# Products on constants in the waits of TensorE, wider landmark products and a later transposition, in a four-layer transformer kernel

## The chip, the cores and the metric

The kernel runs on one core of a Trainium2 chip. The metric is the device time of one execution in microseconds (us), lower is better. TensorE is called PE below, VectorE DVE, ScalarE ACT, GpSimd POOL and SyncE SP.

## What is computed

The input x has 4 sequences of 512 rows of 128 numbers, all in fp32. Six residual layers follow each other:

```python
x = x + 0.5 * L0_ffn(layernorm(x))    # 8 dense experts of 128 hidden units, weights from a sigmoid router
x = x + L0_attn(layernorm(x))         # 16 heads of 8, 64 landmarks, 6 Newton steps for an inverse
x = x + 0.5 * L0_ffn(layernorm(x))
x = x + 0.5 * L1_ffn(layernorm(x))    # 32 experts, top 4 of each row, and 4 shared experts
x = x + L1_attn(layernorm(x))         # windows of 128 keys, 7 windows a sequence
x = x + 0.5 * L1_ffn(layernorm(x))
```

The inverse of the landmark attention starts from V = K^T / denom, where denom is the largest column sum, and repeats V = 0.25 V (13 I - KV (15 I - KV (7 I - KV))). Its result is multiplied with the landmark rows of kernel3 @ v.

## The kernel before

The 2048 rows are held as 16 tiles of 128 rows, in four groups of 512 (one group is one sequence). Every engine has its instructions written out in a fixed order, and semaphores are waited for by hand; whatever stands behind a wait in an engine's order waits too. The program has these stages, with the times at which they lie in the profiled execution:

- **Dense feed-forward, first (0 to 102 us)**, function `ffn0`. 32 steps, eight experts for each of four groups. In step s, PE does `gate_up(s + 1)` (six products of 512 columns, L404 to L406), then what else is due in that step, and then `down(s)` (L1324), which waits for DVE's `hidden(s)` (L1237). ACT applies silu and scales the result (L1196), POOL adds it to x (L1122). Routing and normalising (L215) of later groups are pieces in DVE's order, put between two `hidden`. `FOLLOWING` says at which step of the next group the norm of the next stage is done for a finished group.
- **Landmark attention (102 to 307 us)**, `attn0`. After the scores of the landmarks come six Newton iterations for all heads (`times`, L1939, products of 72 columns: 64 of the matrix A and, behind them, 8 of the landmark rows), then `landmark_values` (L1979), products of the 8 last columns alone. With them go `scores1` (L1956), whose row maxima DVE takes (L1770), `turn_maxima` (L1991), and the scores and values of all rows (L2002, L2015, L2018).
- **Dense feed-forward, second, with the routing of the sparse layer (307 to 473 us)**, `ffn0` with `srt`. For each finished group the norm, the router and the ranks of its rows are worked out in steps of the next group (`SOON`, `SPREAD`), and POOL then sends the rows to `sorted_rows` in DRAM by 16 indirect transfers a group (`pool_dispatch`, L455). Their list also has the `power` (L208) on which the norm of the next group waits. Steps 32 to 47 are the shared experts.
- **Tiles of the sparse layer (473 to 607 us)**, `Sorted.tiles`: 20 quads of four tiles. SP and ACT load them, PE transposes (L894), multiplies (L916), transposes (L923), multiplies (L930), DVE weights the rows (L854) and POOL sends them back with four indirect transfers a quad (L731).
- **Window attention with the routing of the last layer (607 to 731 us)**, `attn1`, and **tiles again (731 to 860 us)**, then the last sums and the store.

Two helpers fill waits of PE with products whose result nobody reads:

```python
def keep_busy(n, b):
    for _ in range(n):
        PE.matmul(b[:, 0:3 * D], ident[:, :], wqkv[:, :], start=True, stop=True)
def keep_warm(n, b):
    for _ in range(n):
        PE.matmul(b[:, 0:P], ident[:, :], ident[:, :], start=True, stop=True)
```

They are the lines L176 and L180 of the profile. One product of fp32 is two instructions there, so `keep_busy(1)` is "x2" of L176 and `keep_warm(1)` is "x2" of L180. Both stand in PE's order ahead of a wait.

## Time and profile before

| | us |
|---|---|
| time, median of 3 runs | 877.46 |
| the three runs | 875.30, 877.46, 881.89 |
| the profiled execution | 880.06 |
| its span in the trace | 878.6 |
| mean granted clock of PE | 0.931 |

The span is from the first to the last instruction of the program; 1.5 us of the execution's time lie around it. "PEclk" or "granted clock" is the share of 2.4 GHz that PE's array was allowed to run at. It takes two values in this trace, 1.00 (2.4 GHz) and 0.50 (1.2 GHz); a value between the two is a mean over a stretch that has both. "Idle before" with an arrow names what ended the wait of an engine.

### The profile page before, as it was taken

The page shows a single profiled execution, that of the slowest core. Times are in us where ns is not written, and L with a number is a line of the kernel's source. Part 1 is how long each engine was busy: PE and PEld are TensorE (multiplying, and loading weights), DVE is VectorE, ACT ScalarE, POOL GpSimd, SP SyncE. Part 2 cuts the span into 40 slices and gives each one's busy share as a digit, 9 for nine tenths or more (in the row PEclk, how much of TensorE's full clock was granted, in tenths as well). Part 3 has the DMA queues.
Part 4 walks back from the last instruction along what each step waited for, and adds up shares of the span by engine and source line. Part 5 has one row for each costly group of instructions (what it writes and reads, how often), then busy time and mean ns, then how long its engine had stood idle before and what let it go on. Part 6 is the DMA issues. An engine that isn't in the chain of part 4 may idle for free.

```text
span 878.6 us, 19350 instructions
## 1 busy us (share of the span) xinstructions
PE 724.0 (82%) x6670; PEld 556.0 (63%) x6670; DVE 530.4 (60%) x1596; ACT 401.5 (46%) x971; POOL 446.0 (51%) x489
## 2 busy tenths in 40 slices
PE   7889998889999898888998677875888987788830
PEld 6778856569977567777776455553666774555520
DVE  6975596558856287867782354443876662354524
ACT  3657654556425455455413355640554323455520
POOL 4755530435500046375673367775357771477770
PEclk9999998999978998899999999997998998899985
DMA  9999999480045091011111444425001112344417
GB/s 229 214 216 217 217 214 219 97 160 4 5 101 111 1 324 37 1 46 37 44 56 52 107 105 109 107 79 209 1 31 54 56 57 50 86 109 111 111 52 245
DMA packets 121024, 93.98 MB, mean 107 GB/s; under 512 B 14176, under 2 KB 111840, under 8 KB 120544
## 3 DMA queue, kind: packets, MB, share of 16 engines
q1 hardware_dynamic: 104256, 70.00, 36.1%
q0 software_dynamic: 9216, 19.68, 6.5%
q10 hardware_dynamic: 7456, 3.07, 1.7%
q8 instruction: 54, 0.88, 0.4%
q14 instruction: 42, 0.34, 0.1%
HBM read 31.76 MB, written 57.41 MB: 101 GB/s over the span
## 4 chain that ended last, share of the span: by engine, by line
PE 39%; POOL 16%; DVE 15%; issue 12%; SPq 9%; ACT 5%; DMA 4%; ACTq 1%; DVEq 0%; POOLq 0%
POOL sorted_rows L455 8%; SPq L713 7%; POOL expert_rows L731 7%; PE banks L1939 5%; PE banks L1324 4%; PE banks L404 2%; PE banks L405 2%; PE banks L406 2%; PE banks L916 2%; DVE hT L1237 2%; PE banks L642 1%; PE banks L176 1%; PE banks L1956 1%; PE banks L1900 1%; DVE rows_x L215 1%
## 5 line engine op out<-in xcount | busy, mean ns | idle before, releaser
L731 POOL DMA_INDIRECT expert_rows<-y,goal x160 | 153.2, 957 | 103.9 <-DVE y L854 55.7
L455 POOL DMA_INDIRECT sorted_rows<-rows_x,row_of x128 | 126.4, 987 | 67.2 <-issue 37.2
L1196 ACT ACTIVATE ys<-banks,wtab 128x128 f32<-128x128 f32 x256 | 73.1, 370 | 65.2 <-PE banks L1324 53.5
L916 PE MATMUL banks<-routed_w,t 128*64 x320 | 83.0, 403 | 11.0 <-issue 5.5
L404 PE MATMUL banks<-x_high,w_high 128*128 128x512 f32 x192 | 86.1, 449 | 0.4 <-POOL w_low L1075 0.4
L1324 PE MATMUL banks<-w,hT 128*128 128x128 f32 x512 | 75.2, 293 | 11.1 <-DVE hT L1237 10.9
L916 PE MATMUL banks<-routed_scratch,t 128*64 128x256 f32 x320 | 83.1, 403 | 0.0
L1122 POOL TENSOR_TENSOR x<-ys,x 128x512 f32<-128x512 f32 x43 | 55.5, 1290 | 54.3 <-ACT ys L1196 54.0
L1324 PEld LDWEIGHTS banks<-w,hT 128*128 128x128 f32 x512 | 69.0, 203 | 20.2 <-DVE hT L1237 17.7
L406 PE MATMUL banks<-x_high,w_low 128*128 128x512 f32 x192 | 77.6, 404 | 0.0
L405 PE MATMUL banks<-x_low,w_high 128*128 128x512 f32 x192 | 77.1, 402 | 0.0
L763 ACT COPY routed_scratch<-routed_w 128x384 f32 x160 | 69.8, 509 | 11.2 <-issue 9.0
L208 POOL TENSOR_TENSOR rstd<-rstd,mhalf 128x4 f32<-128x4 f32 x24 | 25.6, 1065 | 96.3 <-DVE rstd L202 96.1
L916 PEld LDWEIGHTS banks<-routed_w,t 128*64 128x64 f32 x320 | 42.5, 143 | 37.2 <-issue 22.3
L1237 DVE TENSOR_TENSOR hT<-sg,banks 128x512 f32<-128x512 f32 x64 | 43.8, 684 | 30.0 <-ACT sg L1204 27.7
L823 DVE COPY t<-banks 128x512 f32<-128x512 f32 x38 | 26.2, 689 | 58.2 <-PE banks L894 54.4
L776 ACT COPY hT<-banks 128x512 f32<-128x512 f32 x38 | 22.2, 585 | 76.4 <-PE banks L923 59.6
L842 DVE TENSOR_TENSOR h<-sg,banks 128x512 f32<-128x512 f32 (+1 forms) x42 | 27.7, 659 | 36.9 <-ACT sg L770 22.1
L1939 PE MATMUL banks<-routed_w 64*64 64x72 f32 x1536 | 48.9, 223 | 0.6 <-DVE routed_w L1755 0.6
L1939 PEld LDWEIGHTS banks<-routed_w 64*64 64x64 f32 x1536 | 48.3, 133 | 1.2 <-DVE routed_w L1755 1.0
L176 PE MATMUL banks<-wqkv,ident 128*128 128x384 f32 x96 | 37.8, 542 | 11.9 <-DMA xnT<-expert_rows 8.9
L930 PE MATMUL banks<-routed_w,hT 128*64 x320 | 44.7, 283 | 1.8 <-ACT hT L776 1.8
(342 smaller groups left out, 1720.4 us busy)
## 6 DMA issues: line engine op xcount, KB each, us to landing
sorted_rows<-zeros SPq DMA_DIRECT2D x32, 1120.0 KB, 17.3
tile<-sorted_rows SPq DMA_DIRECT2D x252, 35.0 KB, 2.0
routed_w<-in_ffn_w SPq DMA_DIRECT2D x8, 768.0 KB, 11.4
w<-in_ffn_w SPq DMA_DIRECT2D x20, 192.0 KB, 5.6
expert_rows<-y,goal POOLq DMA_INDIRECT x160
tile<-sorted_rows ACTq DMA_DIRECT2D x68, 35.0 KB
qS<-x_high SPq DMA_DIRECT2D x8, 256.0 KB, 6.5
sorted_rows<-rows_x,row_of POOLq DMA_INDIRECT x128
```

The source lines that it names most:

```text
L404: PE.matmul(ps, expert.high[:, n, :], x_high[:, cols], start=True, stop=False)
L405: PE.matmul(ps, expert.high[:, n, :], x_low[:, cols], start=False, stop=False)
L406: return PE.matmul(ps, expert.low[:, n, :], x_high[:, cols], start=False, stop=True)
L455: POOL.indirect_dma_start(sorted_rows, bass.IndirectOffsetOnAxis(self.row_of[:, g, i:i + 1], 0), rows_x[:, 4 * g + i // TOPK, :], None).th ...
L713: SP.dma_start(tile[q % 3][ROWS * h:ROWS * h + ROWS, i, :], sorted_rows[bass.ds(row, ROWS), :]).then_inc(*(head_loaded if q == 0 and i > 1 ...
L731: POOL.indirect_dma_start(expert_rows, bass.IndirectOffsetOnAxis(goal[:, 4 * q + i:4 * q + i + 1], 0), y[q % 6][:, i * P:(i + 1) * P], Non ...
L763: last = SCL.copy(odd[q % 3][:, i, :], routed.w[:, bass.ds(expert[4 * q + i], 1), :].rearrange("p o c -> p (o c)"))
L916: last = PE.matmul(pairs(q)[ROWS * h:ROWS * h + ROWS, i, :], t[q % 2][:, rows], weights(q, i, h, slice(0, 2 * P)), start=True, stop=True)
L1196: last = SCL.mul(ys[s % 2][:, j * P:(j + 1) * P], bank[4 + s % 2][:, j * P:(j + 1) * P], wtab[:, t, e:e + 1])
L1237: DVE.tensor_tensor(hT[s % 2][:, :], sg[s % 2][:, :], bank[2 + s % 2][:, :], ALU.mult).then_inc(*hidden_done.inc)
L1324: last = PE.matmul(bank[4 + s % 2][:, j * P:(j + 1) * P], hT[s % 2][:, j * P:(j + 1) * P], experts[s % rows].w[:, 2, :], start=True, stop= ...
L1939: last = PE.matmul(bank[2 * b + k // 4][r, c + cols.start:c + cols.stop], X[r, k, 0:M], X[r, k, cols], start=True, stop=True)
```

## The change

- `Norm.transposes` gets a number of `keep_busy` products, which come after the wait for the free bank and ahead of the wait for the normalised rows. Two are given for group 3 in the second `ffn0`, and 0, 2, 1, 1 for the four groups of the sorted norm there. Elsewhere it is 0 and only the order of its two waits changes.
- `down` of `ffn0` waits for `scaled_done` first, then does 12 `keep_warm` products at step 6 of the first `ffn0` or 18 at step 9 of the second, and then waits for `hidden_done`.
- `FOLLOWING` for group 0: normalised at step 6 in place of 4 of the next group, transposed at 8 in place of 5, copied at 9 in place of 6.
- `landmark_values` multiplies with all 72 columns. The sequences and heads are laid out in reverse order, so that the 64 columns too many of each product fall on places that hold nothing yet or are written again by a later product. `rden`, `evict_w` and the reader of `WV` follow the new layout.
- `keep_busy` is put into `attn0` (1 and 2 products around the second `turn_maxima`, 1 ahead of the last `spread1`, 1 ahead of the last `output`), into both executions of `tiles` (5 in place of 2 ahead of the first tiles, 2 ahead of the second half of quad 0, 3 ahead of quad 2, 2 ahead of quad 3) and into `attn1` (22 in place of 10 at its start, 3 ahead of the last `srt.norm.transposes`).

```diff
@@ -215,10 +215,11 @@
 
-def transposes(self, g):
-    PE.wait_ge(*xn_ready(self.first + g + 1))
+def transposes(self, g, meanwhile=0):
     if self.turn[g]:
         PE.wait_ge(*xT_ready(self.turn[g]))
+    keep_busy(meanwhile, bank[6])
+    PE.wait_ge(*xn_ready(self.first + g + 1))
     for t in range(4):
@@ -934,9 +935,10 @@
         PE.wait_ge(*dispatched(4 * TOPK * NG))
-        keep_busy(2, bank[0])
+        keep_busy(5, bank[0])
         PE.wait_ge(*loaded(0))
         transposes(0, range(2))
+        keep_busy(2, bank[2])
         PE.wait_ge(*head_loaded(4))
@@ -957,6 +959,7 @@
         gate_up_rows(1, range(2, 4))
+        keep_busy(3, bank[1])
         PE.wait_ge(*loaded(2))
@@ -981,6 +984,8 @@
                 gate_up_rows(n, range(2, 4))
+            if n == 2:
+                keep_busy(2, bank[1])
             if n + 1 < QUADS:
@@ -1108,10 +1113,10 @@
 
-FOLLOWING = dict(statistics=1, normalised=4, transposes=5, copy=6)
+FOLLOWING = [dict(statistics=1, normalised=6, transposes=8, copy=9)] + [dict(statistics=1, normalised=4, transposes=5, copy=6)] * 2
 
 def following_at(s, piece):
-    return [g for g in range(NG - 1) if following and s == rows * (g + 1) + FOLLOWING[piece]]
+    return [g for g in range(NG - 1) if following and s == rows * (g + 1) + FOLLOWING[g][piece]]
 
@@ -1317,9 +1322,10 @@
             return srt.tensor_down(s, experts[8:12])
-        PE.wait_ge(*hidden_done(s + 1))
         if s > 1:
             PE.wait_ge(*scaled_done(s - 1))
+        keep_warm({9: 18}.get(s, 0) if srt else {6: 12}.get(s, 0), bank[4 + s % 2])
+        PE.wait_ge(*hidden_done(s + 1))
         for j in range(4):
@@ -1342,13 +1348,13 @@
         if s in transposes_at:
-            norm.transposes(transposes_at[s])
+            norm.transposes(transposes_at[s], 2 if srt and transposes_at[s] == 3 else 0)
         if s in logits_at:
...
         for g in groups_at(s, "transposes"):
-            srt.norm.transposes(g)
+            srt.norm.transposes(g, (0, 2, 1, 1)[g])
         for g in groups_at(s, "logits"):
@@ -1703,7 +1709,7 @@
             DVE.wait_ge(*rden_ready(b))
-            DVE.tensor_tensor(A[b - 1][:, :, 0:M], pv(bank[6]), m8(rden[:, b - 1, :]), ALU.mult).then_inc(*A_ready.inc)
+            DVE.tensor_tensor(A[b - 1][:, :, 0:M], pv(bank[6]), m8(rden[:, B - b, :]), ALU.mult).then_inc(*A_ready.inc)
         if b == B:
@@ -1718,8 +1724,8 @@
             DVE.wait_ge(*ksum_mm(b + 1))
-            DV(DVE.tensor_reduce(out=rden[:, b, :], in_=pv(bank2), axis=AX, op=ALU.max))
-            DVE.reciprocal(rden[:, b, :], rden[:, b, :]).then_inc(*rden_ready.inc)
+            DV(DVE.tensor_reduce(out=rden[:, B - 1 - b, :], in_=pv(bank2), axis=AX, op=ALU.max))
+            DVE.reciprocal(rden[:, B - 1 - b, :], rden[:, B - 1 - b, :]).then_inc(*rden_ready.inc)
 
@@ -1792,7 +1798,7 @@
         DVE.wait_ge(*W_mm(1))
-        w = bank[5][:, 0:B * NK * HD].rearrange("p (b k d) -> p b k d", b=B, d=HD)
+        w = bank[5][:, M:M + B * NK * HD].rearrange("p (b k d) -> p b k d", b=B, d=HD)
         for h, r in enumerate(HALF):
@@ -1973,10 +1979,10 @@
         PE.wait_ge(*turn(next_ready, 6, max(b, 2)))
-        for k in range(NK):
+        for k in reversed(range(NK)):
             for r in HALF:
-                c = b * GH * 2 + k * HD
-                last = PE.matmul(bank[5][r, c:c + HD], K[b][r, k, :], A[b][r, k, M:TC], start=True, stop=True)
+                c = ((B - 1 - b) * NK + k) * HD
+                last = PE.matmul(bank[5][r, c:c + TC], K[b][r, k, :], A[b][r, k, :], start=True, stop=True)
         if b == B - 1:
@@ -2012,7 +2018,7 @@
         for j in range(4):
-            PE.matmul(bank[5][GH * j:GH * j + GH, :], WV[:, b, 2 * j + c, :], e1[2 * j + c], start=c == 0, stop=c == 1)
+            PE.matmul(bank[5][GH * j:GH * j + GH, :], WV[:, B - 1 - b, 2 * j + c, :], e1[2 * j + c], start=c == 0, stop=c == 1)
         for j in range(4):
@@ -2037,7 +2043,9 @@
     scores1(7)
+    keep_busy(1, bank[6])
     turn_maxima(0, 1)
+    keep_busy(2, bank[6])
     for b in range(B + 1):
@@ -2057,6 +2065,8 @@
         ahead(1)
+        if b == B:
+            keep_busy(1, bank[0])
         if b:
@@ -2066,6 +2076,8 @@
         ahead(3)
+        if b == B:
+            keep_busy(1, bank[0])
         if b:
@@ -2354,7 +2366,7 @@
     PE.wait_ge(*earlier.all_but_last)
-    keep_busy(10, bank[5])
+    keep_busy(22, bank[5])
     PE.wait_ge(*earlier.back_here[0])
@@ -2391,6 +2403,7 @@
         if s == LATE["transposes"]:
+            keep_busy(3, bank[5])
             srt.norm.transposes(LAST)
```

## Rows read from the trace of the kernel before

**Rows 1.** Page, part 2: granted clock in 40 slices of 22 us, in tenths

```profile
PEclk9999998999978998899999999997998998899985
```

**Rows 2.** Windows, PE alone: window, its length, PE busy (instructions), granted clock, DMA

```profile
36.60:40.00 3.40, 3.40 (x13) 0.50 1.16 216
251.60:268.70 17.10, 15.22 (x82) 0.50 0.98 196
333.50:340.40 6.90, 6.12 (x24) 0.51 0.00 0
354.00:360.90 6.90, 5.87 (x21) 0.51 0.00 0
750.00:756.80 6.80, 6.08 (x34) 0.50 0.28 67
```

**Rows 3.** Timeline of PE: start, duration, instruction, [idle before, what ended it]; dense layers

```profile
35.15 1.16 PE L1324 MATMUL banks<-w,hT 128*128 128x128 f32 x8 [2.48 <-DVE hT L1237]
59.54 0.66 PE L223 MATMUL banks<-ident,rows_x 128*128 128x128 f32 x4 [3.47 <-DVE rows_x L215]
334.29 1.11 PE L223 MATMUL banks<-ident,rows_x 128*128 128x128 f32 x4 [2.72 <-DVE rows_x L215]
355.03 2.08 PE L1324 MATMUL banks<-w,hT 128*128 128x128 f32 x8 [3.70 <-DVE hT L1237]
384.98 1.12 PE L223 MATMUL banks<-ident,rows_x 128*128 128x128 f32 x4 [2.33 <-DVE rows_x L215]
411.97 2.01 PE L1324 MATMUL banks<-w,hT 128*128 128x128 f32 x8 [0.97 <-DVE hT L1237]
```

**Rows 4.** Timeline of PE around the landmark products

```profile
245.38 1.22 PE L1939 MATMUL banks<-routed_w 64*64 64x72 f32 x32
248.43 1.10 PE L1979 MATMUL banks<-routed_w 64*64 64x8 f32 x32
255.40 0.69 PE L1991 MATMUL banks<-ident,mrow 128*128 128x128 f32 x2 [0.78 <-DVE mrow L1770]
257.18 1.22 PE L2002 MATMUL banks<-qS,x_high 112*128 112x512 f32 x2 [1.09 <-ACT qS L1619]
```

**Rows 5.** Timeline of POOL: where the lists of indirect transfers began

```profile
429.48 1.16 POOL L455 DMA_INDIRECT sorted_rows<-rows_x,row_of  x1 [4.67 <-DVE row_of L507]
469.93 0.96 POOL L455 DMA_INDIRECT sorted_rows<-rows_x,row_of  x1 [0.30 <-issue]
644.88 1.03 POOL L455 DMA_INDIRECT sorted_rows<-rows_x,row_of  x1 [12.08 <-DVE row_of L507]
757.96 0.96 POOL L731 DMA_INDIRECT expert_rows<-y,goal  x1 [6.95 <-DVE y L854]
```

**Rows 6.** Timeline of PE: the products on constants (L180, L176)

```profile
11.72 0.83 PE L180 MATMUL banks<-ident 128*128 128x128 f32 x6
590.94 6.69 PE L176 MATMUL banks<-wqkv,ident 128*128 128x384 f32 x20 [2.32 <-DMA expert_rows<-y,goal]
606.55 7.78 PE L176 MATMUL banks<-wqkv,ident 128*128 128x384 f32 x18 [8.93 <-DMA xnT<-expert_rows]
```

**Rows 7.** Windows, all engines: length, busy PE, PEld, DVE, ACT, POOL, clock, DMA

```profile
40.00:45.00 5.00, 5.00 (x34) 4.43 (x33) 4.86 (x16) 3.48 (x11) 2.12 (x2) 1.00 1.18 219
```

**Rows 8.** Timeline of DVE behind waits of PE, and normalising (L215)

```profile
339.76 0.69 DVE L1237 TENSOR_TENSOR hT<-sg,banks 128x512 f32<-128x512 f32 x1 [1.63 <-PE banks L406]
366.75 0.69 DVE L1237 TENSOR_TENSOR hT<-sg,banks 128x512 f32<-128x512 f32 x1 [1.05 <-ACT sg L1204]
389.30 0.69 DVE L1122 TENSOR_TENSOR x<-ys,x 128x512 f32<-128x512 f32 x1 [2.14 <-ACT ys L1196]
613.11 1.11 DVE L215 TENSOR_SCALAR rows_x<-x,mv,rstd 128x128 f32<-128x128 f32 x4
```

**Rows 9.** Timeline of DVE: maxima of two score tiles

```profile
262.16 1.29 DVE L1770 TENSOR_REDUCE mrow<-banks 128x8 f32<-128x512 f32 x2 [0.29 <-PE banks L1956]
```

**Rows 10.** Waits of PE in the first tiles, 472 to 602: total, times, longest us

```profile
PE banks L894 <- DMA tile<-sorted_rows: 12.6, 8, 2.6
```

## The prediction

> **What bounds the kernel now.** I read the page first. Its line of the granted clock shows 0.9 and full tenths with dips to 0.7 and 0.8 spread over the whole span [rows 1]: PE falls from its upper level (2.4 GHz) to the lower one (1.2 GHz) again and again, and not only in the idle tail. The windows put around these dips show stretches of 3.4, 6.8 and once 17 us with a clock of 0.50, in which PE is busy nearly all the time [rows 2]. So it works at half speed with work at hand. What comes before each fall is read from the timeline of PE: a wait of 2.3 to 3.7 us for DVE or a DMA [rows 3], or, ahead of the long stretch, narrow products of 8 columns [rows 4]. The reader is to see there that the fall comes after the wait, in the next few microseconds, and lasts longer than the wait itself: the wait costs nothing more if it is filled, but the slow work after it may.
>
> Whether a slow PE costs time is a second question, and the chain of waits and DVE's and POOL's timelines answer it. In the two dense layers and the attention the chain goes through PE and DVE in turns. From 429.5 to 470.9 it is POOL, which sends its transfers with 0.30 us between them [rows 5], so 32 transfers and one power in 41 us, whatever PE does. In the window attention POOL takes over at 644.9 in the same way [rows 5], and in the tiles it is the loads by SP and POOL's returns. So I sum only what lies ahead of these points.
>
> **The price of the fillers.** 20 instructions of L176 took 6.69 us, 0.67 us for a product, at full clock [rows 6]. For L180, six took 0.83 [rows 6] and the same form as a transposition took 0.66 for four [rows 3], so a further product costs between 0.17 (2 x 0.085) and 0.28 (0.83 / 3); I take 0.21, as the drain of the last one is paid once. At the lower clock all double.
>
> **First dense layer.** Ahead of `down(6)` PE waits 2.48 [rows 3]; 12 products last 2.0 to 3.3, by my value 2.5: hidden in DVE's work, and 0.8 late at worst. The slow stretch 36.6 to 40.0 (up to half of 3.4, 1.7) goes. DVE is busy 4.86 of the 5 us behind it [rows 7], so little of this arrives: I take 0.6. The moved piece is four normalisations of 1.11 together [rows 8], transpositions of 0.66 that waited 3.47 [rows 3] and one copy by ACT, which was busy 3.48 of 5 us here [rows 7]; no DMA and no transfer of POOL belongs to it, and SP's queue isn't touched. It leaves DVE's order ahead of `hidden(13)`, which so comes 1.1 earlier, and goes in ahead of `hidden(15)`, still behind the routing pieces of steps 13 and 14, so that `hidden(15)` is as late as before. PE's transpositions, now in step 16, add 0.6 ahead of `down(16)` but wait for nothing, ACT's copy in step 17 likewise. I put it at 0, between -1.1 and +0.7. The wait of 3.47 isn't filled and remains 2.4 to 3 us long; the clock may still fall here.
>
> **Landmark attention.** 32 instructions took 1.10 with 8 columns and 1.22 with 72 [rows 4]: 4 x 0.12 = 0.5 us more. In the 45 us of Newton products of 72 columns ahead of it no dip is seen [rows 1], and with those of 8 the clock falls at 251.6 [rows 2]. With the waits of 0.78 and 1.09 [rows 4] covered by one and two products (0.67 and 1.34, 0.2 too long), I expect full clock through to the scores. Half of 15.22 busy us [rows 2] would be 7.6 gained. DVE stops it: it takes 12 maxima there at 1.29 for two [rows 9], 7.7 us, with small gaps 8.3. Behind 257.2, 11.5 slow us become 8.3 and 0.9 for the value products, 2.3 gained; the first scores come 0.5 earlier, and the last landmark and score products, slow before, give back 1.0 against the 0.5 of wider products. Together 3.3. The two single products at the last sequence lie in waits for DVE; what runs slow behind them is one stretch as long as that at 36.6 [rows 2], mostly fillers already: I take 0.5 of at most 1.7.
>
> **Second dense layer.** Four waits, all ahead of POOL's 429.5:
> - 334.29: 2.72 waited, two products (1.34) lie in it. 6.12 busy us at half clock [rows 2] hold 3.1. DVE behind it waited 1.63 for PE [rows 8], and again at the next step, so most arrives: 2.3.
> - 355.03: 3.70 waited, 18 products last 3.1 to 5.0, by my value 3.8: 0.1 late, 1.3 at worst. Half of 5.87 is 2.9; DVE's idle time behind it, 1.05 [rows 8] and a shorter one a step earlier, is the room: 1.7.
> - 384.98: 2.33 waited, two products (1.34). PE then takes 1.12 for transpositions that take 0.66 at full clock [rows 3], DVE waits 2.14 behind it [rows 8]: 1.45.
> - 411.97: 0.97 waited [rows 3], and about as long ahead of the group's transpositions, where one product (0.67) now lies. `down` takes 2.01 in place of 1.16 [rows 3]: 1.55 of at most 1.7.
>
> Together 7.0. The product for group 3 is behind 429.5; it delays PE by up to 0.7 while POOL sets the end.
>
> **Tiles and window attention.** In the first tiles PE waited for loads eight times, 2.6 us at longest and 12.6 in all [rows 10]. The three products more ahead of quad 0, and the two, three and two behind it (2.0, 1.3, 2.0, 1.3), are no longer than that; the first may be some tenths late, but the second half of quad 0 waits for a load of its own. I take 0. In the second tiles POOL was idle 6.95 ahead of quad 1 [rows 5] while PE ran at half clock, 750.0 to 756.8 [rows 2]; quad 3 then waits for its own load again, so of 3 us (half of 6.08) I let 0.8 through. In the window attention 22 products last 14.7, from 590.94 to 605.7, and the wait ends at 606.55 [rows 6]. The nine behind them took 7.78, partly slow [rows 6], and take 6.0: done at 612.6, but DVE's normalised rows come at 614.2 [rows 8]. So this largest filler buys nothing. Its cover is the wait for the returned rows and then the 1.6 us of DVE's; beyond them each product would cost 0.67. The three ahead of the last norm (2.0) meet a wait of 0.7 and delay PE by 1.3, behind 644.9, where POOL is the bound: 0.
>
> **The sum.** 0.6 + 0 + 3.3 + 0.5 + 7.0 + 0 + 0.8 = 12.2. Against the profiled execution: 880.06 - 12.2 = 867.9 (span 878.6 to 866.4). That execution lies 2.6 above the median, and an average run of before had fewer dips to lose; from the median the same sum would give 865.3. I take 867.0, between.
>
> In the sum only part of a slow stretch arrives: of 6.12 slow us at 333.5 I let 2.3 through, since DVE is next. The Trainium skill, "TensorE: Matmul & The Clock Gate", section "Terms", puts the penalty at the throttled time times (1 - K/N), which is half of it here. By that rule the five stretches of [rows 2], 41.1 us, would alone give back 20.5, and the kernel would take 859.5.
>
> **The rivals.**
> 1. All slow busy time comes back: DVE and ACT follow PE everywhere, so that nothing of the slow stretches is cover for them. For it speaks DVE's idle time in the second dense layer, against it the full DVE at 40 to 45 [rows 7]. Halves of the busy times in [rows 2]: (3.40 + 15.22 + 6.12 + 5.87 + 6.08) / 2 = 18.3, with 3.0 and 0.5 for the others 21.8, so 858. Chance 0.08. It is where the page's rule leads.
> 2. The dips move: a wait left as it is (59.54, the loads, the attention's first scores), which the profiled execution passed at full clock or slow by chance of how work lay, takes the place of those filled, or the array falls again where a filler covers only half. Half of 12.2: 874 from the profiled execution, 871.4 from the median. Chance 0.16, inside 1%.
> 3. The change does not do what it says: the clock falls at the same places, as the wide landmark products and half-filled waits aren't enough. The fillers are hidden, 0.5 is lost: 878. Chance 0.08.
> 4. On the other side: the 22 products meet a slow array. The wait of 2.32 ahead of 590.94 [rows 6] lets the clock fall, and a product costs 1.34: 31 of them last 41.5, longer than the 23.3 between 590.94 and 614.22, 18 us on the path that feeds POOL at 644.9. 867 + 18 = 885. It decides once more than 3 of the 31 run slow: 23.3 - 31 x 0.67 = 2.5 us of spare cover, and 0.67 more for each; past 22 of them the whole gain is gone. The 20 before it ran fast after the same wait [rows 6], which speaks against. Chance 0.04.
>
> **How the numbers follow.** My forecast has 0.64, with 862 to 872 as its own range; the small terms (0.8 and 1.3 late fillers, -1.1 to +0.7 for the moved piece, 2 to 4.5 for the attention) make this width. About 1% is what a measurement of this kernel can tell from no change; faster by that is below 868.7. Some three quarters of the forecast (0.50) and rival 1 (0.08) lie there: 0.58. Slower is rival 4, 0.04. The rest, 0.38, is within 1%. The range 860 to 874 leaves out rivals 1, 3 and 4, together 0.20.
>
> **What would show it.** A clock of 1.00 from 245 to 268, at the transpositions of group 3 and behind step 9 of the second dense layer; POOL's third list starting near 418 in place of 429.5 and its last transfer near 459; DVE with less idle time there; the 22 products ending ahead of the first returned rows. The prediction would be wrong if `down` still takes 2 us at these places, if fillers end behind the release of their wait, or if POOL's list starts earlier and the end doesn't follow.

## The result and the profile after

The kernel before took 876.42 us (median of 20 runs, 871.46 to 885.51), the changed one 870.68 (20 runs, 865.27 to 877.60). The ratio is 0.9928, with a 95% interval of 0.9898 to 0.9957: 5.7 us less, within 1%. In a second measurement (`after_again` below) it was 0.9953 (0.9926 to 0.9979). The forecast was 867.0 with a range of 860 to 874; its sum of 12.2 us is about twice what came. The median lies in the forecast's own range of 862 to 872, but nearer to the 871.4 of rival 2 than to 867.0, and that of the second measurement, 873.85, lies outside it. Ratios, and the medians of the experiments, leave out slow executions (over 1.5% above the fastest of their kernel).

The profiled execution of the changed kernel took 873.04 us, its span is 871.2. The granted clock in 40 slices, to be held against [rows 1]:

```profile
PEclk9999999699999999999999999999998998999985
```

Between 36 and 480 us one slice is below 0.9, the eighth, and the kernel before had 0.9 there (a stretch of 3.4 us at 59.8 is too short to show). The windows, first at the places of [rows 2] (its first four; they lie 1.4 us later to 7.4 us earlier now), then at that new dip. Columns: window, its length, busy us of PE, PEld, DVE, ACT and POOL with their instructions, granted clock, DMA share, GB/s:

```profile
34.00:40.00 6.00, 6.00 (x49) 5.68 (x48) 5.83 (x23) 2.46 (x7) 3.99 (x4) 1.00 1.16 215
245.00:268.00 23.00, 22.23 (x316) 17.05 (x314) 15.23 (x31) 8.12 (x12) 0.00 (x0) 1.00 0.53 108
327.00:334.00 7.00, 5.09 (x27) 3.56 (x27) 6.89 (x13) 2.85 (x8) 5.27 (x5) 1.00 0.56 198
347.00:354.00 7.00, 7.00 (x57) 6.65 (x56) 6.72 (x29) 1.95 (x7) 4.01 (x4) 1.00 0.00 1
155.40:169.00 13.60, 13.60 (x104) 10.69 (x104) 7.95 (x12) 5.28 (x13) 4.15 (x4) 0.50 0.27 52
```

The fillers of the second dense layer in PE's timeline, and the rows that answer to [rows 3]. Columns here and in all timelines: start, us, engine, line, operation, tiles, shapes, instructions, and in brackets the idle time before them with what ended it:

```profile
330.48 1.45 PE L176 MATMUL banks<-wqkv,ident 128*128 128x384 f32 x4
333.32 0.65 PE L224 MATMUL banks<-ident,rows_x 128*128 128x128 f32 x4 [1.39 <-DVE rows_x L215]
348.57 4.18 PE L180 MATMUL banks<-ident 128*128 128x128 f32 x36
378.08 1.45 PE L176 MATMUL banks<-wqkv,ident 128*128 128x384 f32 x4
379.89 0.66 PE L224 MATMUL banks<-ident,rows_x 128*128 128x128 f32 x4 [0.36 <-DVE rows_x L215]
```

The products for the two groups lie inside the waits that they were meant for (1.39 and 0.36 us are left), and the work behind all of them runs at full clock. The 18 products ahead of step 9 do not lie inside theirs. They take 4.18 us, 0.23 for one, and end at 352.75; `down` starts without any idle time, while DVE had released it 0.9 us before:

```profile
350.96 0.69 DVE L1242 TENSOR_TENSOR hT<-sg,banks 128x512 f32<-128x512 f32 x1
352.59 1.06 PE L1330 MATMUL banks<-w,hT 128*128 128x128 f32 x8
```

It cost nothing here, since DVE has no idle time between 351 and 360. POOL's third list, [rows 5] with its 429.48, and the first two quads of the second tiles, where [rows 5] has an idle time of 6.95:

```profile
422.09 1.16 POOL L456 DMA_INDIRECT sorted_rows<-rows_x,row_of  x1 [3.11 <-DVE row_of L508]
...
462.55 0.96 POOL L456 DMA_INDIRECT sorted_rows<-rows_x,row_of  x1 [0.30 <-issue]
...
749.33 0.96 POOL L732 DMA_INDIRECT expert_rows<-y,goal  x1 [4.26 <-DVE y L855]
```

**Where the time went.** Both programs have the same instructions on DVE, and in the same order but for the four moved normalisations (between 50 and 66 us, inside the first column), so each can be timed in both traces. The sheet below is worked out from the traces in that way. A column is the stretch between two instructions of DVE, named by the times at which they start in the first profile of the kernel before, and a number is how much longer the stretch is than in that profile. All fourteen profiles of this study are in it; the experiments are described below.

```
                        first   score   land-  second  first   window  last   second
                        dense   stage   mark   dense   tiles   attn.   norm   tiles
                       20-95   95-232 232-309 309-443 443-590 590-690 690-700 700-870
before (first profile)   0.00    0.00    0.00    0.00    0.00    0.00    0.00    0.00
before_again             0.11   -2.74    1.37   -2.85    0.33    0.63   -0.01   -0.44
second_dense_alone      -0.12   -2.66   -2.33   -6.35    1.64    0.25    0.02    0.80
landmark_alone          -0.82    1.91   -4.37   -2.68   -1.06   -0.09   -0.01   -1.30
changed kernel          -0.03    1.96   -4.36   -6.33   -0.02    0.25    0.79   -1.02
after_again              0.01    1.86   -4.08   -5.77    3.18    0.20    1.07   -0.71
second_dense_unfilled    0.50    0.05   -4.08   -2.98   -0.86   -0.35    1.07   -2.53
two_parts_undone         1.56   -1.20   -4.05   -6.32   -0.80    2.19    0.01   -1.97
scores_filled            2.15   -0.43   -4.36   -6.36   -0.75    2.27    1.35   -3.71
scores_filled_again     -0.16    3.61   -4.08   -6.42    1.00   -0.08    0.02   -1.33
narrow_landmark         -0.16    3.98   -2.04   -5.74    0.40    0.27    0.76   -2.40
short_filler             2.20    3.53   -4.06   -6.34    1.65    0.27    0.02   -2.50
tiles_unfilled           2.31   -0.43   -4.38   -6.32    1.75    0.20    1.15   -2.66
fitted_fillers           0.55    1.13   -4.08   -6.31   -0.09    0.97    0.02   -2.39
```

In the profiled pair the landmark stage and the second dense layer are 4.4 and 6.3 us shorter, nearly the sum of 12.2. Against them stand 1.4 at the start (weights that landed later: ACT waits 2.08 us for them in place of 0.25, ahead of anything that the change touches), 2.0 in a score stage that the change doesn't touch, and 0.8 ahead of the last norm. The total is 7.4 of span.

### The profile page after: what moved, and what is told of

Read it like the earlier page. It is cut to its first block, busy times and chain, and to the rows that moved or that the text cites. A ratio compares the mean times of both kernels' runs of the same rounds, so it can differ in the third digit from the quotient of the medians.

```text
span 871.2 us, 19648 instructions
## 1 busy us (share of the span) xinstructions
PE 739.1 (85%) x6822; PEld 563.3 (65%) x6822; DVE 533.9 (61%) x1596; ACT 401.7 (46%) x971; POOL 445.5 (51%) x489
## 3 DMA queue, kind: packets, MB, share of 16 engines
q10 hardware_dynamic: 7456, 3.07, 1.6%
## 4 chain that ended last, share of the span: by engine, by line
PE 40%; DVE 21%; POOL 13%; issue 13%; DMA 5%; ACT 4%; SPq 2%; ACTq 2%; DVEq 0%; POOLq 0%
POOL sorted_rows L456 8%; PE banks L1945 5%; PE banks L917 5%; POOL expert_rows L732 4%; PE banks L1330 3%; DVE hT L1242 2%; SPq L714 2%; PE banks L405 2%; PE banks L407 2%; PE banks L406 2%; PE banks L1906 2%; DVE rows_x L215 2%; PE banks L643 1%; PE banks L176 1%; PE banks L1871 1%
## 5 line engine op out<-in xcount | busy, mean ns | idle before, releaser
L1201 ACT ACTIVATE ys<-banks,wtab 128x128 f32<-128x128 f32 x256 | 73.3, 370 | 66.4 <-PE banks L1330 54.4
L917 PE MATMUL banks<-routed_w,t 128*64 x320 | 79.9, 392 | 11.3 <-issue 5.8
L405 PE MATMUL banks<-x_high,w_high 128*128 128x512 f32 x192 | 84.0, 437 | 1.7 <-POOL w_low L1080 1.7
L1330 PE MATMUL banks<-w,hT 128*128 128x128 f32 x512 | 71.0, 282 | 11.7 <-DVE hT L1242 11.6
L917 PE MATMUL banks<-routed_scratch,t 128*64 128x256 f32 x320 | 80.0, 392 | 0.0
L1330 PEld LDWEIGHTS banks<-w,hT 128*128 128x128 f32 x512 | 64.8, 193 | 20.9 <-issue 11.5
L407 PE MATMUL banks<-x_high,w_low 128*128 128x512 f32 x192 | 75.8, 395 | 0.0
L176 PE MATMUL banks<-wqkv,ident 128*128 128x384 f32 x188 | 67.5, 500 | 3.1 <-DMA expert_rows<-y,goal 1.7
L176 PEld LDWEIGHTS banks<-wqkv,ident 128*128 128x128 f32 x188 | 34.5, 193 | 25.0 <-issue 4.5
## 6 DMA issues: line engine op xcount, KB each, us to landing
sorted_rows<-zeros SPq DMA_DIRECT2D x32, 1120.0 KB, 17.1
```

Source lines behind the costliest of these rows:

```text
L405: PE.matmul(ps, expert.high[:, n, :], x_high[:, cols], start=True, stop=False)
L407: return PE.matmul(ps, expert.low[:, n, :], x_high[:, cols], start=False, stop=True)
L917: last = PE.matmul(pairs(q)[ROWS * h:ROWS * h + ROWS, i, :], t[q % 2][:, rows], weights(q, i, h, slice(0, 2 * P)), start=True, stop=True)
L1201: last = SCL.mul(ys[s % 2][:, j * P:(j + 1) * P], bank[4 + s % 2][:, j * P:(j + 1) * P], wtab[:, t, e:e + 1])
L1330: last = PE.matmul(bank[4 + s % 2][:, j * P:(j + 1) * P], hT[s % 2][:, j * P:(j + 1) * P], experts[s % rows].w[:, 2, :], start=True, stop= ...
```

## The experiments

**A second look at the kernel before** (`before_again`, no edit).

> The unchanged kernel, for a second profile of it. Question: are the falls of TensorE's clock fixed in place or do they come by chance? Theory A (chance): the changed kernel gains 12 us when the falls of the first profile are there and less when they are not, so at least two of the seventeen stretches with a granted clock of 0.50 of the first profile (36.6, 60.5, 135.6, 251.6, 306.2, 333.6, 354.0, 384.8, 412.1 and so on) are missing or lie elsewhere here, and the span differs by the busy time they held. Theory B (fixed): the same stretches come within 2 us of their places, and the difference of 6 us between the sum and the median result has another cause.

Its stretches at half clock: 36.4 to 39.8, 60.3 to 63.7, 248.0 to 268.5, 306.0 to 309.4, 333.3 to 336.7, 353.8 to 357.2, 384.5 to 387.9, and others from 476.7 on. Those at 135.6 and 412.1 are missing, and two in the second dense layer are half as long:

```profile
135.00:142.00 7.00, 6.40 (x68) 4.41 (x66) 4.35 (x7) 3.19 (x8) 0.00 (x0) 1.00 0.97 210
333.30:340.10 6.80, 6.17 (x36) 5.87 (x37) 5.78 (x31) 2.89 (x9) 1.27 (x1) 0.75 0.00 0
353.80:360.60 6.80, 6.80 (x37) 5.84 (x35) 6.49 (x34) 4.26 (x12) 3.02 (x3) 0.75 0.00 0
411.00:415.00 4.00, 4.00 (x29) 3.67 (x28) 2.21 (x8) 2.39 (x7) 3.09 (x4) 1.00 0.17 58
```

The same program, with the same waits, gave its second dense layer 2.8 us back and its score stage 2.7. So theory A holds: whether the clock falls behind a wait differs between executions of one program. The first profile, from which my sum was made, was a costly one in these two stages; in the landmark stage the second is the costlier, by 1.4 (a fall of 20.5 us in place of 17.1). The timed runs agree. Over 76 runs of the kernel before in the three sets, time and mean granted clock go together (correlation -0.43, -0.74 and -0.78 in the sets, 3.2 to 5.0 us for 0.01 of clock; 4.7 over all). A hundredth of clock over 876 us is 17.5 us at half speed, so some 0.27 of the slow time is paid for, an estimate.

**The landmark part alone** (`landmark_alone`): the kernel before with

```diff
-                            last = PE.matmul(bank[5][r, c:c + HD], K[b][r, k, :], A[b][r, k, M:TC], start=True, stop=True)
+                            last = PE.matmul(bank[5][r, c:c + TC], K[b][r, k, :], A[b][r, k, :], start=True, stop=True)
...
+                keep_busy(1, bank[6])
                 turn_maxima(0, 1)
+                keep_busy(2, bank[6])
```

and what belongs to it (the order of the columns, the two products in the last sequence).

> The kernel before with one part of the change: landmark value products of 72 columns and the five products around the maxima and in the last sequence. Theory A (each part gives what its place shows): no stretch of 0.50 between 245 and 268; against the kernel before the stage is 3.3 to 3.9 us shorter up to the first scores of the attention, and the time falls by 2 to 4 us (ratio 0.995 to 0.998), less where the runs of the kernel before pass the place at full clock. Theory B (the gain of the whole change comes from the second dense layer only): ratio 0.999 to 1.001.

Measured: 873.01 us against 874.29, ratio 0.9978 (0.9955 to 1.0). No fall between 245 and 268; the stage is 4.4 us shorter than in the first profile of before. That is theory A for the stage. The time agrees with it, but its interval reaches theory B's 0.999 to 1.001.

**The second dense layer's part alone** (`second_dense_alone`): the kernel before with `keep_busy` ahead of the groups' transpositions and 18 products of `keep_warm` ahead of step 9.

> The kernel before with another part alone: the products ahead of the group transpositions and of step 9 in the second dense layer. Theory A: the stretches of 0.50 at 333.6, 354.0, 384.8 and 412.1 are gone, GpSimd's third list starts 6 to 7 us earlier, and the time falls by 5 to 7 us (ratio 0.992 to 0.994): GpSimd sets the end from there. Theory B (what is gained there is given back later, in the tiles or the window attention, because another fall of the clock or a load takes over): the third list starts 6 us earlier, but the time falls by 0 to 3 us.

Measured: 872.25 against 874.29, ratio 0.9981 (0.9950 to 1.0012), 1.7 us with an interval from 1 us longer to 4.4 shorter. The layer is 6.35 us shorter than in the first profile, as theory A said, but the time is not: theory B's number. Part of the riddle is solved by `before_again`, whose untouched layer is 2.85 shorter too; another part is in this profile's first tiles, 1.6 longer.

**The new dip filled** (`scores_filled`, and `scores_filled_again` as the base of the next three): the changed kernel with six products ahead of the wait for a slot of transpositions.

```diff
                     if i > 1:
+                        if i % 4 == 1:
+                            keep_warm(6, bank[i % 4])
                         PE.wait_ge(*slot_free(i))
```

The place in the changed kernel, a wait and the slow work behind it:

```profile
151.71 0.66 PE L1906 MATMUL banks<-ident,sg 128*128 128x128 f32 x4
153.75 0.63 PE L1906 MATMUL banks<-ident,sg 128*128 128x128 f32 x4 [1.38 <-ACT xnT L1598]
154.31 1.13 PE L1871 MATMUL banks<-routed_scratch 32*128 32x512 f32 x4
155.37 1.97 PE L1879 MATMUL banks<-routed_w 64*64 64x64 f32 x32
157.27 3.67 PE L1889 MATMUL banks<-routed_w,routed_scratch 128*128 128x64 f32 x16
```

and the same wait in `before_again`, which fell nowhere here (L1883 is the line of L1889):

```profile
134.77 0.63 PE L1900 MATMUL banks<-ident,sg 128*128 128x128 f32 x4 [1.37 <-ACT xnT L1592]
135.33 1.13 PE L1865 MATMUL banks<-routed_scratch 32*128 32x512 f32 x4
136.39 1.15 PE L1873 MATMUL banks<-routed_w 64*64 64x64 f32 x32
137.47 2.00 PE L1883 MATMUL banks<-routed_w,routed_scratch 128*128 128x64 f32 x16
```

> The changed kernel with six products of 128 columns more in four places of the first attention's score stage, ahead of the wait for the slot of the transpositions of items 1, 5, 9 and 13 (1.38 us long in both profiles, with slow work behind it: 137 to 142 before, 157 to 168 after). Theory A (falls of the clock in waits that nobody fills are what is left of the spread between runs): no stretch of 0.50 between 120 and 200, the time 1 to 4 us below the changed kernel's, and its runs lie closer together. Theory C (VectorE and ScalarE set the pace of this stage whatever TensorE's clock): the stretch is gone and the time is the same, or 0 to 1 us longer since the six products last up to 1.2 us in a wait of 1.4.

> The changed kernel with the score stage filled, run again as the base of the three others of this set and for a second profile. Theory A: no stretch of 0.50 between 90 and 440 again, a median of 867 to 870 and a spread of less than half of the 16 us of the kernel before. Theory B (the narrow spread was luck): the falls and the spread are back.

Measured: 868.57 against 874.29 (ratio 0.9909, 0.9881 to 0.9936) and 871.74 against 878.25 (0.9933, 0.9903 to 0.9962), the runs 865.66 to 870.00 and 869.83 to 874.00. There is no fall between 120 and 200, and the runs lie closer together (4.3 and 4.2 us from lowest to highest; the kernel before 7.9 and 12.7, the changed kernel 12.3 in its first 20 runs and 7.2 in `after_again`). That the falls filled here are the reason isn't shown: `narrow_landmark` below has its landmark fall back and spreads over 4.8. My expectation of no fall from 90 to 440 missed one at 203 in the second profile (below). The expected gain of 1 to 4 us isn't there for sure; the changed kernel itself was not run in these two sets, so only ratios to the kernel before can be compared (0.9928 and 0.9953 without the six products). The trace says why. The six products cost 2.3 us of their own: DVE's instructions in this stage come 0.36, 0.43, 0.25, 1.02 and 0.25 later at five of the seven places, whose waits are 0.7 and 0.9 us or none, where the products last 1.5. I had written four places; there are seven. Only the two waits of 1.38 hold them.

**The width of the landmark products** (`narrow_landmark`): that base with `HD` columns again in place of `TC` (the diff of above reversed), the fillers kept.

> The same kernel with the landmark value products of 8 columns again in place of 72, the products around the maxima kept. Theory A (the width holds the clock): a stretch of 0.50 of 10 to 17 us between 245 and 270, and the time 3 to 4 us above the base. Theory D (the products that fill the waits at the maxima are what holds it, width is idle cost): full clock there, and the time 0.5 us below the base, since 32 products take 1.10 and not 1.22 us four times.

Measured: 876.25 us against the base's 871.74, and means that differ by 4.4 (+- 1.2). PE in the narrow one:

```profile
250.91 1.10 PE L1987 MATMUL banks<-routed_w 64*64 64x8 f32 x32
252.37 1.10 PE L1987 MATMUL banks<-routed_w 64*64 64x8 f32 x32
253.84 1.35 PE L1987 MATMUL banks<-routed_w 64*64 64x8 f32 x32
255.84 1.88 PE L1987 MATMUL banks<-routed_w 64*64 64x8 f32 x32
...
259.10 1.48 PE L176 MATMUL banks<-wqkv,ident 128*128 128x384 f32 x2
```

and the same place in the changed kernel:

```profile
250.28 1.22 PE L1985 MATMUL banks<-routed_w 64*64 64x72 f32 x32
251.86 1.22 PE L1985 MATMUL banks<-routed_w 64*64 64x72 f32 x32
...
256.97 0.81 PE L176 MATMUL banks<-wqkv,ident 128*128 128x384 f32 x2
```

With 8 columns the clock falls at 254.5, in the third batch and ahead of any wait, for 6.8 us; with 72 it stays. PE is busy at that point in both. One profile could be chance, but the others agree: in all four profiles with 8 columns the clock falls here (at 248.0, 248.7, 251.6 and 254.5), and in none of the ten with 72. So the width holds the clock, theory A, and the fillers alone don't. The fall is shorter than the 10 to 17 us that I expected. In the sheet 2.0 of the 4.4 us are in the landmark stage and 0.7 right behind it; this profile doesn't show where the rest is.

**The largest filler** (`short_filler`):

```diff
-                keep_busy(22, bank[5])
+                keep_busy(10, bank[5])
...
-                        keep_busy(3, bank[5])
                         srt.norm.transposes(LAST)
```

> The same base with 10 products in place of 22 in the window attention's largest filler and without the three ahead of the last norm's transpositions. My account: their cover is the returned rows and VectorE's normalised rows, so the time is that of the base within 1 us, even if a stretch of 0.50 appears at 600 to 610; the three lie ahead of products that feed GpSimd and cost up to 1.3. Rival: the filler is worth its length, and the time is 2 to 3 us above the base.

Measured: 871.88 against 871.74, means 0.6 apart (+- 1.5). The two edits together make no difference that these runs can tell. In the profile the clock falls at 588.3 and 601.9, and PE waits 6.22 us between its ten and its nine products, yet the window attention is as long as in the changed kernel (0.27 against 0.25 in the sheet): the twelve products more buy nothing. In the changed kernel:

```profile
583.51 14.43 PE L176 MATMUL banks<-wqkv,ident 128*128 128x384 f32 x44 [1.71 <-DMA expert_rows<-y,goal]
599.16 6.07 PE L176 MATMUL banks<-wqkv,ident 128*128 128x384 f32 x18 [1.22 <-DMA xnT<-expert_rows]
606.97 0.63 PE L224 MATMUL banks<-ident,rows_x 128*128 128x128 f32 x4 [1.74 <-DVE rows_x L215]
```

All 31 run at full clock, 1.22 and 1.74 us of wait are left behind them: the spare cover of 2.5 that I had worked out is 3.0.

The column "last norm" of the sheet is a finding that the time of this run is too coarse for. The seven profiles with the three products ahead of the last norm have 0.02 to 1.35 there, 0.89 on average; the seven without have -0.01 to 0.02. The rows, first the changed kernel, then `short_filler` at its own times:

```profile
683.49 2.10 PE L176 MATMUL banks<-wqkv,ident 128*128 128x384 f32 x6
685.42 0.60 PE L224 MATMUL banks<-ident,rows_x 128*128 128x128 f32 x4
```

```profile
690.64 0.63 PE L224 MATMUL banks<-ident,rows_x 128*128 128x128 f32 x4 [0.84 <-DVE rows_x L215]
```

The wait is 0.84, the products take 2.10. That is DVE's time. Whether it reaches the end is read from POOL, whose transfers the second tiles wait for. From its first transfer of this stage to its last, at 721.88 in the changed kernel, it is never idle for more than 0.4 us, in any of the fourteen profiles, with the three products or without:

```profile
637.60 1.03 POOL L456 DMA_INDIRECT sorted_rows<-rows_x,row_of  x1 [12.14 <-DVE row_of L508]
...
721.88 0.95 POOL L456 DMA_INDIRECT sorted_rows<-rows_x,row_of  x1 [0.30 <-issue]
```

So POOL's list covers most of the delay. Its last 32 transfers take 40.20 to 40.26 us in the seven profiles without the products and 40.23 to 40.89 in those with them: 0.0 to 0.7 more, 0.35 on average. The last column of the sheet gives the difference back, as DVE's next instructions wait for these transfers.

**The tiles' products** (`tiles_unfilled`): the base without the ten that the change adds.

> The same base without the ten products that the change adds in the tiles (three and two and three and two). My account: 0 in the first tiles, 0.8 in the second, so 0 to 1.5 us above the base. Rival (the products delay what comes behind them: a load's quad is transposed up to 2 us late): 0.5 to 2 us below the base. Third: the waits for loads let the clock fall in either kernel (both profiles have stretches of 0.50 at 480 and 736), and the time is the same within 0.5.

Measured: 872.58 against 871.74, means 1.5 apart (+- 1.7). It can't tell my account from the third. In the sheet both tile columns are those of the other runs.

**Two suspects undone** (`two_parts_undone`), beside the changed kernel on the same chip (`after_again`):

```diff
-            FOLLOWING = [dict(statistics=1, normalised=6, transposes=8, copy=9)] + [dict(statistics=1, normalised=4, transposes=5, copy=6)] * 2
+            FOLLOWING = [dict(statistics=1, normalised=4, transposes=5, copy=6)] * 3
...
-                    keep_warm({9: 18}.get(s, 0) if srt else {6: 12}.get(s, 0), bank[4 + s % 2])
+                    keep_warm({9: 18}.get(s, 0) if srt else 0, bank[4 + s % 2])
...
-                        keep_busy(3, bank[5])
                         srt.norm.transposes(LAST)
```

> The changed kernel itself, as the base of the three others of this set and for a second profile of it. Expected: 5 to 7 us below the kernel before; from VectorE's instruction at 232 us of the kernel before to the one at 309 it is 4.1 to 4.4 us shorter and from 309 to 443 6.4 us shorter than in the first profile of before, as in every run with these parts so far. In the first dense layer (52 to 95 us) it is either as long as before, with the clock's fall at 60, or 2.4 us longer, with the fall at 67; in the score stage (125 to 232) it depends on chance whether a fall costs 0, 2.7 or 4.7 us.

> The changed kernel without two of its parts, in stages far apart: the first dense layer's (the moved rows of group 0 and the twelve products ahead of step 6), and the three products ahead of the last norm's transpositions. Theory E (these two parts lose what the others gain): between 52 and 95 us no loss of 2.4 us and no wait of 2.8 us ahead of step 15's down projection; between 690 and 700 us the 0.8 to 1.3 us that the runs with the three products lose are gone; the time is 1 to 2.5 us below the changed kernel's. Theory F (the prediction's 0 for both): the same time within 0.5.

Measured: the changed kernel 873.85 (0.9953), without the two parts 868.64 (6 runs; 0.9907, 0.9871 to 0.9942), means 4.9 apart (+- 2.5). It is the fastest median beside `scores_filled`. For the three products the profile agrees (0.01 in place of 1.07 on DVE, and POOL's last 32 transfers 40.20 in place of 40.83). For the first dense layer it doesn't: this one execution was slow there from 59.5 to 66.4 and is 1.56 us longer. The profiles together say more. Those with the moved rows have two values, about 0 (0.01, -0.03, -0.16, -0.16, 0.50) and about 2.2 (2.15, 2.20, 2.31). The down projections of `scores_filled` (dear) and of `scores_filled_again` (cheap):

```profile
58.92 1.13 PE L1330 MATMUL banks<-w,hT 128*128 128x128 f32 x8 [3.05 <-DVE hT L1242]
61.28 1.05 PE L1330 MATMUL banks<-w,hT 128*128 128x128 f32 x8
66.51 1.30 PE L1330 MATMUL banks<-w,hT 128*128 128x128 f32 x8 [2.78 <-DVE hT L1242]
```

```profile
59.23 1.74 PE L1330 MATMUL banks<-w,hT 128*128 128x128 f32 x8 [3.05 <-DVE hT L1242]
63.18 1.05 PE L1330 MATMUL banks<-w,hT 128*128 128x128 f32 x8
66.02 1.13 PE L1330 MATMUL banks<-w,hT 128*128 128x128 f32 x8 [0.40 <-DVE hT L1242]
```

Both wait 3.05 us ahead of step 13. In the second the clock falls at 59.6, PE is slow while DVE is busy with the routing, and nothing is lost. In the first it doesn't fall, PE runs ahead, waits 2.78 for `hidden(15)`, ahead of which the moved normalisations now stand, and falls at 67.3, where DVE follows it: 2.3 us. Not all of this is the fall's. In `fitted_fillers` (below) the clock falls nowhere here, and 0.7 us are lost all the same: `hidden(15)` starts at 66.00 there, 65.69 in the first execution above and 65.19 in the second, since one normalisation ahead of it takes 1.18 us in place of 0.35. So 1.6 are the fall's, of at most 1.7 (half of 3.4). One fall, 3.4 us long both times, costs nothing that can be seen at one step and 1.6 two steps later. The five profiles without the part have 0.00, 0.11, -0.12, -0.82 and 1.56; the -0.82 is `landmark_alone`, which has no fall here at all, so by this one profile a fall at 60 costs some 0.7 in the kernel before. The averages, 0.85 with and 0.15 without, speak for a loss of 0.7; they are too few to show it, and what the other 3 to 4 of the 4.9 us are I can't say.

**A version with fitted fillers** (`fitted_fillers`):

```diff
+                        keep_warm({5: 6, 9: 2, 13: 6, 17: 2, 21: 3, 29: 3}.get(i, 0), bank[i % 4])
                         PE.wait_ge(*slot_free(i))
...
-                    keep_warm({9: 18}.get(s, 0) if srt else {6: 12}.get(s, 0), bank[4 + s % 2])
+                    keep_warm({9: 18}.get(s, 0) if srt else {6: 12, 13: 12, 15: 10}.get(s, 0), bank[4 + s % 2])
```

and with the edits of `short_filler`.

> A version meant to beat both. The changed kernel with: in the score stage, in place of six products each, as many as each wait holds (6, 2, 6, 2, 3, 0, 3: the even six cost 0.36, 0.43, 0.25, 1.02 and 0.25 us in the four profiles that have them, 2.3 in all); in the first dense layer twelve and ten products in the waits of 3.05 and 2.78 us ahead of steps 13 and 15; ten products in place of 22 and none ahead of the last norm. Expected: no stretch of 0.50 from 20 to 440, the score stage 2.7 us shorter than in the first profile of before (2.4 without all of the fit), the first dense layer as long as before in every run, and a median 3 to 5 us below the changed kernel's, 9 to 11 below before, with a spread of less than 8 us. Rival: the products in the first dense layer end late or the clock falls a step later, and it is no faster than the changed kernel.

Measured: 869.87 against the changed kernel's 873.85 (ratio to before 0.9929, 0.9901 to 0.9956), means 3.2 apart (+- 1.8), all runs within 4.7 us. The windows at both sides of its one fall:

```profile
20.00:195.00 175.00, 166.79 (x1435) 128.91 (x1436) 121.32 (x304) 104.20 (x285) 79.39 (x103) 1.00 1.06 192
205.00:440.00 235.00, 219.98 (x2752) 182.94 (x2749) 176.80 (x549) 117.98 (x279) 101.49 (x95) 1.00 0.25 69
```

Full clock for 410 us, and the products of the score stage now cost nothing: up to 200 us DVE's instructions come 0.3 to 0.4 earlier than in profiles without products and falls here, in place of 2.2 later. The version gains 3 to 5 on the changed kernel as expected, but is no better than the one that leaves two parts out: the 9 to 11 below before that I expected came out as 7.7.

**What comes at 200 us.** Seven of the fourteen profiles have a wait there that no fill explains, 2.45 us in `scores_filled_again`, 2.83 in `fitted_fillers` and, in `after_again`:

```profile
196.20 3.59 PE L1945 MATMUL banks<-routed_w 64*64 64x72 f32 x106 [0.26 <-DVE routed_w L1761]
203.01 3.19 PE L1945 MATMUL banks<-routed_w 64*64 64x72 f32 x52 [3.22 <-issue]
```

PE waits for nothing that the profile shows, at the start of the Newton products. Windows from 198 to 202, one of `after_again`, one of the changed kernel's first profile:

```profile
198.00:202.00 4.00, 1.79 (x56) 1.64 (x52) 2.54 (x8) 3.09 (x6) 3.02 (x3) 1.00 1.19 189
```

```profile
198.00:202.00 4.00, 3.69 (x98) 3.26 (x91) 2.56 (x14) 0.27 (x1) 0.00 (x0) 1.00 0.02 6
```

In the seven with the wait the DMA share of this window is 0.52 to 1.19, since the large transfers of zeros into `sorted_rows` are still running; in the seven without it is 0.01 to 0.31. They need not run through the wait itself: in `two_parts_undone` and `short_filler` the share is 0.07 to 0.12 while PE stands, and the transfers end just before. The wait costs 1.5 to 4.6 us by 232, with what follows it. That the instructions come late because the transfers are in their way is a possible reading, and no experiment here tests it. The wait is in all four profiles of the last set and in three of the four before, sets in which the kernel before was 3 to 4 us slower than in the first set as well. It is in none of the six earlier profiles, two of which have the whole change. That speaks for the set and not for the change, but no profile of the kernel before was taken in those two sets, and all seven with the wait are of the changed kernel or variants of it.

**The second dense layer again, from the other side** (`second_dense_unfilled`): the changed kernel without that layer's products.

> The changed kernel without the products in the second dense layer. Theory A: the stretches near 330, 350, 381 and 408 are back, or some of them; 309 to 443 takes 2.7 to 6.4 us more than in the changed kernel (three profiles without these products had 0, 2.8 and 2.7 us less than the first profile of before, those with them 6.4 less); the time is 3 to 6 us above the changed kernel's. Theory B (later stages take it back, as the run with this part alone seemed to say with 1.7 us): 0 to 2 us above it.

Measured: 872.66 against 873.85, means 0.1 apart (+- 2.5): theory B. The profile has the falls (311, 332, 352 and 407; 3.4 us each) and the layer is 2.8 us longer than in `after_again`, the tiles 4.0 shorter. With this part (ten profiles) the layer has -5.7 to -6.4, and the first tiles 0.8 on average. Without it (four profiles) the layer has 0, -2.9, -2.7 and -3.0, and the first tiles -0.4 on average. So 4.1 is gained and 1.2 of it given back in the tiles, 2.9 in all, though the first tiles scatter from -0.8 to 3.2 among the ten. The timings are 1.7 with this part alone, whose interval holds 2.9, and -0.1 (+- 2.5) here, whose interval ends just short of it. Whether anything of this largest term reaches the end is left open.

## Why the prediction came out as it did, by its own steps

- **The falls and what cures them.** Right. The clock is 1.00 at all places named up to 480 us, and rivals 1, 3 and 4 are out. One of the signs of being wrong came all the same: the 18 products end some 1 us behind the release of their wait (0.23 for one, where I took 0.21), at no cost since DVE was busy. POOL's third list began at 422.1 and ended at 462.6, not near 418 and 459; the 1.4 at the start and the 2.0 in the score stage are most of that. Rival 2 is there in part: the new stretch at 155.4 to 169.0 behind a wait that the change doesn't fill (it cost 4.6 us in that run, the old one at 135.6 had cost 2.7), and the moved fall in the first dense layer. It is no transfer of falls, though, since `landmark_alone`, which fills nothing here, has it as well, and `before_again` has none.
- **Landmark, 3.3 + 0.5.** Measured 4.1 to 4.4 in ten profiles against the first of before, 3.9 against the mean of three profiles without. The half microsecond for wider products and the limit by DVE were right, and it is the one term whose gain a comparison of times bears out (4.4 +- 1.2 for the width; for the part alone, ratio 0.9978, the interval reaches 1.0).
- **Second dense layer, 7.0.** Measured 6.3 against the first profile, in nearly every run. This is the step that was too large: as a term for an average run it is 4.1, since the three other profiles without the fillers were 2.7 to 3.0 us cheaper. I had the point in a sentence ("an average run of before had fewer dips to lose") and gave it 2.6 us by the median. The profiled execution had four falls of 20.5 us together in this layer, the others 10.2 to 13.6.
- **First tiles, 0.** The term is about +1.2: POOL's list is 7.4 us earlier, its first return 6.1. That the fillers aren't it is read from one profile (`tiles_unfilled`, 1.75 without them).
- **First dense layer, 0.6 + 0.** The fall at 36.6 is gone and gave 0.2. The moved piece I put at 0, up to +0.7; the failed step was that `hidden(15)` "is as late as before". It is, but PE now waits for it (2.78 us, where `landmark_alone` waits 0.83), and such an execution is 2.3 longer, 1.6 of it by the fall behind the wait. The wait of 3.47 remained as 3.07, as written.
- **The last norm, 0.** Right in the mechanism and near in the size. The delay is as worked out (2.0 in a wait of 0.7, 1.3 late; 0.9 on DVE on average), and so is the cover: POOL is the bound behind 644.9 and is never idle up to its last transfer. What gets through is 0.0 to 0.7, 0.35 on average.
- **Window attention, 22 products, 0.** Right, with the cover as worked out.
- **Second tiles, 0.8.** POOL's idle time went from 6.95 to 4.26, and 1.0 came through. But `tiles_unfilled` has 4.60, so the gain isn't the fillers'; it is the clock's chance in the first profile. The last column is 0.7 to 3.7 us shorter in all ten profiles that hold most of the change, and -1.3 to 0.8 in the other four. Up to 1.3 us of it is what the column ahead of it had lost on DVE only; for the rest I have no cause.

The five terms above, by averages of profiles with and without their part: -3.9 - 4.1 + 1.2 + 0.7 + 0.35 = -5.75 us. The two measurements gave -5.7 and -3.8 by their medians. That the numbers meet is partly luck, since two columns that differ as much are left out: the score stage (+2.3 on average with the change, by falls and waits that differ between executions) and the last one (-1.9). The sum of 12.2 was nearly right for the execution it was made from (10.7 in the two large stages), and wrong for the median. That 870.68 lies in the range is owed to the range's width, not to the sum: 12.2 below the 876.42 of all runs would be 864.2.

In size, a slow stretch cost 2.7 of its 6.8 us in the score stage and 4.6 of 13.6, nothing or 1.6 of 3.4 in the first dense layer, 6.3 of 20.5 in the second. The rule of the Trainium skill ("TensorE: Matmul & The Clock Gate", section "Terms"), by which half of the throttled time is lost, is an upper bound in these stages, where the 1.6 comes close to it; the 76 runs give 0.27.

## What to carry to other kernels

Whether the clock falls behind a wait is chance from run to run, so a slow stretch seen in one profile has to be priced as its cost times how often it occurs: profile the same program two or three times before summing what fillers bring. A filler must be no longer than its wait, priced one by one: six products in a wait for two cost 0.4 us each time, three in a wait of 0.84 delayed DVE by 0.9 on average. Then ask what the delayed engine feeds: there POOL's list of transfers covered all but 0.35 of it. Where the next engine is busy, a slow TensorE is free or nearly so; where the clock holds at that place, TensorE runs ahead, and the next wait may have a fall behind it that isn't free.

## What was not expected of the hardware

- Products of 8 columns, back to back and with PE busy all the time, let the clock fall at 254.5, in the third batch, after Newton products at full clock; 72 columns in the same time (1.22 in place of 1.10 us for 32 instructions) don't.
- PE stood still for 1.6 to 3.2 us with nothing to wait for that the profile shows, early in the Newton products, in all seven executions with a DMA share of 0.52 or more from 198 to 202 us, and in none of the seven with 0.31 or less.
- The same wait of 3.05 us led to a fall in one execution and to none in another.
